# Two layers of attention over 32 images: where the turned maxima are written, when queries are scaled, and how the last image is finished

## The reference

```python
x = x + L0(_gn(x))   # _gn: group norm, 32 groups of 8 channels, no weights
x = x + L1(_gn(x))
```

```python
s = einsum('bhqe,bhke->bhqk', q, k) * scale
s = where(mask, s, finfo.min); p = softmax(s); o = einsum('bhqk,bhke->bhqe', p, v)
out = einsum('bnd,od->bno', o, Wo)
```

## Time and profile before

| what | value |
|---|---|
| time, median of 3 runs | 1193.71 us (1193.16 to 1195.25) |
| time of the profiled execution | 1191.12 us |
| its span, first to last instruction | 1189.3 us |
| TensorE busy in the span | 1118.1 us (94%) |
| VectorE busy | 929.3 us (78%) |
| ScalarE busy | 642.9 us (54%) |
| GpSimd busy | 199.4 us (17%) |
| mean granted TensorE clock | 0.981 |

### The profile page before, as it was taken

One profiled execution on the slowest core, in us unless ns is written; L12 is line 12 of the kernel. 1 busy time (PEld: TensorE's weight loads), 2 busy tenths in 40 slices (PEclk: granted clock), 3 DMA queues, 4 the chain that ended last, 5 costly groups with the idle time before them and its releaser, 6 DMA issues. The chain is left out here.

```text
span 1189.3 us, 50917 instructions
## 1 busy us (share of the span) xinstructions
PE 1118.1 (94%) x21342; PEld 826.0 (69%) x21342; DVE 929.3 (78%) x1669; ACT 642.9 (54%) x1051; POOL 199.4 (17%) x271
## 2 busy tenths in 40 slices
PE   6899999999999999988999999999999999999993
PEld 3677777777777777776667777777777777777762
DVE  5478888888888888856687887878787878787863
ACT  4456666666666666543555555555555555555550
POOL 1001111111111111111222212122221212222220
PEclk9799999999999999999999999999999999999996
DMA  2111111111111110000122222231322222222233
GB/s 87 50 33 44 41 37 37 37 37 37 37 37 37 37 38 24 24 23 10 29 49 62 54 54 58 49 70 40 69 41 66 43 64 45 63 45 62 45 70 75
DMA packets 189150, 55.49 MB, mean 47 GB/s; under 512 B 151172, under 2 KB 184214, under 8 KB 189078
## 3 DMA queue, kind: packets, MB, share of 16 engines
q1 hardware_dynamic: 182584, 52.92, 18.5%
q10 hardware_dynamic: 6496, 1.53, 0.6%
HBM read 35.95 MB, written 18.35 MB: 46 GB/s over the span
## 5 line engine op out<-in xcount | busy, mean ns | idle before, releaser
L1385 DVE TENSOR_REDUCE cm<-psG 128x4 f32<-128x1024 f32 (+1 forms) x192 | 234.9, 1224 | 115.0 <-PE psG L1109 114.9
L1255 ACT ACTIVATE probs<-psG 128x1024 f32<-128x1024 f32 x192 | 196.2, 1023 | 134.5 <-PE psG L1087 134.1
L1087 PE MATMUL psG<-stack 32*128 32x256 f32 (+1 forms) x2048 | 218.4, 342 | 8.7 <-DVE cm L1385 8.0
L1463 POOL TENSOR_SCALAR_AFFINE_SELECT probs<-probs 128x1024 f32<-128x1024 f32 x128 | 139.2, 1099 | 478.2 <-ACT probs L1255 478.1
L1096 PE MATMUL psG<-stack 32*128 32x256 f32 (+1 forms) x2048 | 219.3, 342 | 0.0
L1087 PEld LDWEIGHTS psG<-stack 32*128 32x128 f32 x2048 | 150.2, 185 | 65.7 <-DVE cm L1385 27.5
L1096 PEld LDWEIGHTS psG<-stack 32*128 32x128 f32 x2048 | 149.6, 185 | 1.3 <-issue 0.9
L885 POOL TENSOR_TENSOR X<-X,probs 128x96 f32 (+5 forms) x128 | 54.9, 459 | 482.4 <-ACT probs L625 482.4
L500 PE MATMUL psA<-probs,xh 128*128 128x512 f32 x256 | 126.8, 619 | 2.8 <-ACT xh L658 1.6
L1148 PE MATMUL psA<-xh,wqk 128*128 128x256 f32 x512 | 121.9, 382 | 0.0
L1411 DVE RECIPROCAL stack<-stack 128x128 f32<-128x128 f32 x128 | 115.7, 929 | 4.6 <-DMA stack<-totals 4.6
(11 more groups left out here) (139 smaller groups left out, 1813.1 us busy)
## 6 DMA issues: line engine op xcount, KB each, us to landing
X<-in_xr SPq DMA_DIRECT2D x32, 256.0 KB, 3.8
probs<-inverses SPq DMA_DIRECT2D x32, 256.0 KB
stack<-scratch_heads SPq DMA_DIRECT2D x32, 256.0 KB
stack<-totals SPq DMA_DIRECT2D x64, 128.0 KB
out<-X SPq DMA_DIRECT2D x32, 256.0 KB, 3.0
scratch_heads<-stack SPq DMA_DIRECT2D x124, 64.0 KB
totals<-stack SPq DMA_DIRECT2D x124, 4.0 KB
inverses<-rd SPq DMA_DIRECT2D x32, 32.0 KB, 1.5
```

The source lines that it names most:

```text
L1087: last = nc.tensor.matmul(G[:, to:to + b.size], km[i.k][own_rows(r), o, e, b.keys_of(o) * P:(b.keys_of(o) + 1) * P], qm[i.k][own_rows(r), ...
L1255: nc.scalar.activation(weights[i.k][:, b.weights_at:b.weights_at + 1024], G[:, base:base + 1024], ACT.Exp).then_inc(exp_done, 1)
L1385: nc.vector.reduce_max(slots, scores, AX_X).then_inc(max_done, 1)
L1463: nc.gpsimd.affine_select(out=diagonal, in_=diagonal, compare_op=ALU.is_ge, fill=0.0, base=0, pattern=[[0, QUADS], [0, 2], [sign, P]], cha ...
```

## The change

On TensorE `turn_c` goes behind `project` half 1 and writes the bank E; it waits for the reciprocal of the sums. The wait of `scores` for `ct` goes between its two groups of products. On ScalarE `copy_c` reads E and goes behind the second square. On VectorE `unit_qk` goes ahead of the first half of the bias. The last `output` of layer zero goes behind the last bursts. The last image's statistics go from the end of layer zero to the end of step 0 of layer one. The last image's outputs get a buffer of their own, their copies no longer wait for the stores before, and their eight stores are issued half by ScalarE and half by SyncE.

```diff
@@ def scores(i):
-                wait(pe, c_out, i.count(1))
                 wait(pe, exp_done, i.plus(-1).count(2))
...
                                                  qt[i.k][own_rows(r), o, win(w)], start=(o == 0 and w == 0), stop=False,
                                                  tile_position=(r * COL, e * WTOK), skip_group_check=True)
+                wait(pe, c_out, i.count(1))
@@ def turn_c(i):
                 wait(pe, max_done, i.count(2))
+                wait(pe, r_done, i.plus(-1).count(1))
+                if first(i):
+                    pe.wait_ge(a_tab, 1)
                 for t in range(TT):
-                    last = nc.tensor.transpose(G[:, t * P:(t + 1) * P], cm[:, t, :], ident[:, :])
+                    last = nc.tensor.transpose(E[:, t * P:(t + 1) * P], cm[:, t, :], ident[:, :])
@@ pipeline(pe, ...)
-            [... (only(LAST, bounds_begin), -1), (output, -1), (only(LAST, bounds_end), -1), (turn, 2), ...
-             (lambda i: project(i, 0), 3), (groups, 4, 1), (turn_c, 1), (lambda i: project(i, 1), 3)]
+            [... (only(LAST, bounds_begin), -1), (only(LAST, bounds_end), -1), (output, -1), (turn, 2), ...
+             (lambda i: project(i, 0), 3), (groups, 4, 1), (lambda i: project(i, 1), 3), (turn_c, 1)]
@@ def copy_c(i):
-                nc.scalar.activation(ct[:, :], G[:, 0:TOKENS], ACT.Copy, scale=-1.0).then_inc(c_out, 1)
+                nc.scalar.activation(ct[:, :], E[:, 0:TOKENS], ACT.Copy, scale=-1.0).then_inc(c_out, 1)
@@ pipeline(act, ...)
-             (lambda i: square(i, 0), 3), (bias_within, 1), (copy_c, 1), (lambda i: square(i, 1), 3)]
+             (lambda i: square(i, 0), 3), (bias_within, 1), (lambda i: square(i, 1), 3), (copy_c, 1)]
@@ def later_bounds():
                 later.take_max(WHOLE_1B)
-                stats_next(Image(0, LAST))
-                later.halves(1)
@@ pipeline(dve, ...)
-             (outputs, -1), (lambda i: add_bias(i, 0), 0), (unit_qk, 2), (prepare_bounds, 2), ...
+             (outputs, -1), (unit_qk, 2), (lambda i: add_bias(i, 0), 0), (prepare_bounds, 2), ...
@@ layer one
+    ots_last = flat[0][:, QUADS * TOKENS:2 * QUADS * TOKENS].rearrange("p (g t) -> p g t", g=QUADS)
+    def regroup_half(queue, n):
+        i = Image(0, images - 1)
+        queue.wait_ge(loaded[i.k], i.plus(-2).dmas(LOADS))
+        queue.wait_ge(ot_out[0], images)
+        queue.wait_ge(ot_out[1], images)
+        for c in (2 * n, 2 * n + 1):
+            queue.dma_start(scratch[i.k]...[:, c], ots_last[COL * c:COL * c + DIM, :, :]...).then_inc(stored[i.k], 16)
+        for g in (2 * n, 2 * n + 1):
+            queue.dma_start(totals[i.k]...[g], ots_last[DIM:P:COL, g, :]...).then_inc(stored[i.k], 16)
@@ def regroup(i):   # SyncE
             if here(i, images - 1):
+                regroup_half(sp, 1)
                 return
@@ def copy_outputs(i, o):
-            wait(act, stored[1 - i.k], i.plus(-1).dmas(STORES))
+            if not here(i, images - 1):
+                wait(act, stored[1 - i.k], i.plus(-1).dmas(STORES))
+            to = ots_last if here(i, images - 1) else ots
@@ ScalarE, in the place of regroup_last
+            regroup_half(act, 0)
@@ def last_statistics():   # VectorE, only(0, ...) at the end of the list of layer one
+            dve.wait_ge(l0.x1_done, 4 * images)
+            for c in range(CT):
+                nc.vector.bn_stats(stats2[:, images - 1, c, :], X[:, images - 1, c, :]).then_inc(l0.stats_done, 1)
+            halves(1)
```

More of the change, by code:

```diff
@@ L532, in bounds_end @@
                 later.burst(WHOLE_1B)
-            pipeline(pe, images, [(scores, 0), (project_v, 1), (bounds, 1), (only(LAST, bounds_begin), -1), (output, -1), (only(LAST, bounds_end), -1), (turn, 2), (only(LAST - 1, later.project_first), 0),
+            pipeline(pe, images, [(scores, 0), (project_v, 1), (bounds, 1), (only(LAST, bounds_begin), -1), (only(LAST, bounds_end), -1), (output, -1), (turn, 2), (only(LAST - 1, later.project_first), 0),
                                   (only(LAST, later.project_second), 0), (weigh, 0), (table_read, 0), (sums, 0), (only(LAST, lambda: later.burst(WHOLE_0)), 0),
-                                  (lambda i: project(i, 0), 3), (groups, 4, 1), (turn_c, 1), (lambda i: project(i, 1), 3)], LAGS, once={-3: hide_early, -2: hide_late, -1: tabulate})
+                                  (lambda i: project(i, 0), 3), (groups, 4, 1), (lambda i: project(i, 1), 3), (turn_c, 1)], LAGS, once={-3: hide_early, -2: hide_late, -1: tabulate})
             later.rest()
@@ L663, in _ @@
                                    (only(LAST - 1, later.queries_keys), 0),
-                                   (only(LAST, later.second_queries_keys), 0), (copy_o, 0), (lambda i: square(i, 0), 3), (bias_within, 1), (copy_c, 1), (lambda i: square(i, 1), 3)], LAGS, once={-3: rectify_early, -2: rectify_late, -1: open_table})
+                                   (only(LAST, later.second_queries_keys), 0), (copy_o, 0), (lambda i: square(i, 0), 3), (bias_within, 1), (lambda i: square(i, 1), 3), (copy_c, 1)], LAGS, once={-3: rectify_early, -2: rectify_late, -1: open_table})
             later.rest()
@@ L1232, in scalar, with regroup_first_half @@
     def scalar(act, l0):
[L1233 to L1244, removed]
+        def regroup_first_half():
+            regroup_half(act, 0)
         def exponent(i, b):
@@ L1299, in rest @@
                                    X_(HALVES), (lambda i: copy_outputs(i, 1), -1),
[L1300 removed]
+                                       (only(images - 1, regroup_first_half), -1), (copy_v, 1), X_(HALVES_B), (copy_q, 2),
                                    X_(WHOLE_1), (lambda i: copy_k(i, 0), 2), X_(WHOLE_1B)], LAGS, start=0)
@@ L1439, in rest @@
                                    R(HALVES), I_(1), I_(2), R(HALVES_B), I_(3), (divide, -2), R(WHOLE_1),
-                                   (lambda i: fold_bound(i, 0), 1), (residual, -2), R(WHOLE_1B), (only(2, lambda: roots(1)), 0)], LAGS, start=0)
+                                   (lambda i: fold_bound(i, 0), 1), (residual, -2), R(WHOLE_1B), (only(0, last_statistics), 0),
+                                       (only(2, lambda: roots(1)), 0)], LAGS, start=0)
         return VectorOpening(halves, group_sums, roots, factors, lambda: normalize(first), lambda: normalize(second),
```

11 lines of the change are left out of this document (8 added, 3 removed).

## The result

The changed kernel takes 1213.85 us, median of 4 runs (1213.46 to 1214.44), beside 1194.01 us (1193.16 to 1195.25, 4 runs) for the kernel before: ratio 1.0166, 95% interval 1.0148 to 1.0183. It is 1.7% slower, where 1185.9 us and 0.7% faster was forecast. The span of the profiled execution grew from 1189.3 to 1212.7 us, 23.4 us.

What follows compares the result with a forecast made beforehand. TensorE was taken as nearly full in layer zero's loop, its small waits winnable. Terms -5.5 - 0.2 (written-out steps) - 0.5 + 0.2 - 0.4 - 1.4 = -7.8 us put the median at 1185.9 us, range 1181 to 1191.

Steps and rivals of the forecast that it cites:

- The loop term: Layer zero's 22 loop steps: moving `turn_c` behind `project` 1 saves 0.25 us a step, -5.5 us (0 to -9.9).
- Rivals 1 to 3: Loop: ring not shortened, 1191.4 us (chance 0.14); wait inside `scores` bites, 1203.7 (0.08); more than one wait goes, 1176.0 (0.08).
- the ring: Layer zero's step as a dependency chain over TensorE, ScalarE and VectorE; `turn_c` holds it up 0.25 us a step.
- Both edits are needed together: Loop: moving `turn_c` and putting unit queries ahead of the first bias give 0.25 us a step only together.
- The wait in the middle of `scores`: Loop: `ct` awaited between the two product groups of `scores` arrives with 0.5 us to spare, cost 0.
- Rival 2: Loop: the wait inside `scores` bites, losing 1.07 us there, +10 us in all, 1203.7 us; chance 0.08.
- First image: First image of layer zero: first half of `scores` runs in its wait for `ct`, -0.5 us (0 to -1.9).
- Last two images: Layer zero, no projection to hide behind: `turn_c` waits for the reciprocal, +0.2 us (-0.5 to +0.8).
- The seam: Between layers: last bursts move up 0.85 us, output fills the wait before the full burst, -0.4 us (0 to -1.6).
- The tail: End of kernel: own buffer and split store issue let the last reciprocals start earlier, -1.4 us (-0.5 to -1.7).

Runs made afterwards that it cites:

- after_shift251: The changed kernel with 502 more waits (251 instructions) at the head of TensorE's program; 1235.56 us, ratio 1.0338.
- after_lean: The changed kernel without three TensorE waits that other waits ahead of them already cover; 1193.28 us, ratio 0.9960.
- before_shift5: The kernel before with ten more waits (five instructions) at the head of TensorE's program; 1195.23 us, ratio 1.0004.
- before_unit: The kernel before with only VectorE's order changed, unit queries and keys ahead of the first half of the bias; 1223.29 us, ratio 1.0237.
- before_lean: The kernel before without two covered TensorE waits, in `scores` and `bounds`; 1221.12 us, ratio 1.0188.
- lean_shift8: after_lean with eight extra instructions (16 waits) far ahead of the image loop; 1213.03 us, ratio 1.0150.
- lean_seam_back: after_lean with the last image's output again ahead of the second part of its bounds; 1187.48 us, ratio 0.9931.
- best: lean_seam_back with the last two images' turned maxima in the first bank again and `ct` awaited ahead of `scores`; 1185.82 us, ratio 0.9915.

## Why the prediction was wrong

**The loop term (-5.5 us; measured +17.3).** This step failed, and in two ways. The larger is not in it at all: TensorE loads nine blocks of its own code again in three turns, 20.4 us over quiet steps (with the loop's end short of the edge: 20.3 less). The prediction said of the loop that TensorE "is nearly full, but its small waits are what a reordering can win"; that the loop's 1707 instructions only just stay loaded wasn't seen, and no rival held it. Rivals 1 to 3 are all about waits between engines. What could have been seen blind: 56 packets of 16.4 KB for a program that contains a loop of seven blocks, none loaded twice, and hence something to lose.

The smaller: `turn_c` is worth 0.33 us a pair, not 0.50. From `weigh` to where `project` 1 ends takes 5.69 us instead of 5.95, as counted. But from there to the next `weigh` takes 8.76 and 9.31 instead of 8.67 and 9.21 us, since the square now starts 0.20 us behind the start of what follows `project` 1, not 0.10; the ring gives back 0.09 us a step. Over 22 steps -3.6 rather than -5.5; the six loops without slow groups and with the changed order came to -2.6 to -3.1, as their first pair was longer.

**"Both edits are needed together" was wrong.** The pairs are 29.44 and 29.45 us with either order on VectorE. In the kernel before the unit order alone gives no shorter pair; it sets off the loading.

**The wait in the middle of `scores`, cost 0:** right. No idle before L404 in the loop, and no sign of the few tenths of a us that the prediction held possible there, without a working: 126 products take 1.56 us in after, 124 took 1.53 before. Rival 2 forecast a slower kernel (1203.7 us) by a mechanism that didn't happen.

**First image (-0.5; measured -1.3):** right in sign, too small, within its range. The table's cut hides it, since `scores` now starts ahead of its wait. From the start of `project` half 0 to the bound's products (L404) it is 8.9 to 9.0 us in the five traces with the old order, 7.7 in the nine with the new. TensorE's instructions, before, then after:

```profile
51.32 1.96 PE L500 MATMUL psA<-probs,xh 128*128 128x512 f32 x4 [1.25 <-ACT stack L632]
...
60.35 0.42 PE L404 MATMUL psG<-ct,pick 32*64 32x256 bf16 x1
```
```profile
54.57 1.96 PE L500 MATMUL psA<-probs,xh 128*128 128x512 f32 x4 [0.72 <-ACT stack L635]
...
62.24 0.42 PE L404 MATMUL psG<-ct,pick 32*64 32x256 bf16 x16 [2.03 <-ACT ct L651]
```

The first products run in the wait, which leaves 2.03 us of the 3.09. That `project` itself starts 3.25 us later in after is no part of the change: it starts at 51.0 to 54.8 us with either order (after_shift251, with its longer head, aside).

**Last two images (+0.2):** the mechanism came, its price is open. `turn_c` waits 0.85 us for the reciprocal, twice. The five steps behind the loop take 70.3 to 75.5 us in the seven traces with that wait (mean 72.9), 70.4 to 71.9 in the seven without (mean 71.2), so the change may cost more than was forecast. But in the last of these steps the bound's products come 3.9 us behind the start of `sums` with the wait and 4.0 without, and "issue" of up to 2.15 us inside `scores` moves about from trace to trace; no run separates the two. The 1.92 us of "issue" ahead of L404 in one of the written-out steps of after is such a one (none to 2.00 us elsewhere, 1.23 in before).

**The seam (-0.4; measured +4.0).** The order of events came as forecast, its clock did not. In after_lean the moved bursts start at 539.34; with the lengths of the earlier trace rows at full clock the full burst would follow at 539.34 + (547.02 - 1.57 - 540.60) + 2.05 = 546.24, and it came at 551.24. The step that failed is the silence on the gap: where the output stood ahead of the bursts it filled TensorE's wait for the maximum, and I took only that the bursts "can move up by 0.85". With the output behind, TensorE idles there (1.67 us in after, 1.82 in after_lean), the granted clock falls, and bursts and output run at half speed. Over all traces that is 3.2 us. In after itself 2.2 of the +4.0 lie behind the first burst; the other 1.8 lie ahead of it, at the output that waits 4.34 us and in the projection behind it, and also vary among traces with the same order.

**The tail (-1.4; measured -1.1):** right, by its own mechanism: reciprocals right behind the residual. One term was too small: 0.2 us was taken off because the earlier stores share the DMA engines with image 30's fetch. Image 30's reciprocals start 6.5 to 6.9 us behind the last products at L1129 in the four traces with the old tail, and 6.7 to 9.0 (mean 7.7) in the ten with the new stores, 1.0 us later.

Without the slow groups and with the seam and the last images undone, the kernel comes to 1185.8 us, but by other terms than the forecast's.

**What stays open.** Why timing matters across the edge: before (end 5576) and before_shift5 (5581) load nothing twice, before_unit (5576) and before_lean (5573) load nine blocks in every second turn. The edge itself is only bracketed, between 5569 and 5573. With edges every 256 instructions from there, a loop that ends short of it lies in seven blocks and one that ends behind it in eight. That the sequencer asks for the block behind the loop and so loses the loop's first one fits every run, and the times of the packets (one, less than a microsecond later the next, then seven spread over the two steps that follow), but no packet names its block. Nor is it shown how many turns load again in a run without a trace: of each kernel one run was traced, and the runs of before reach 1203.07 us where the traced one took 1191.12.

## What to carry to other kernels

Read the packets of the instruction queue before and after a change to a kernel with a large unrolled loop: packets over the program's size are code loaded again, and equal products torn apart by 2 us of "issue" are how it looks on the engine. If a loop only just stays loaded, its place matters more than what is in it, and a change on another engine can set it off; shift it by a few instructions, and keep its end clear of the edge, before you judge a reordering. And a long operation that stands in a wait is worth more than the place that it takes: behind it the wait comes back, and with it the clock.

## What the runs showed of the hardware

One reload is nine packets and costs the loop 5.3 us (before_unit: 354.25 - 327.76 = 26.5, five of them) to 7.1 us (lean_shift8: 14.1, two). TensorE's program is that of before in before_unit. The cost is in part the clock: behind the waits of 1.92 and 2.59 us in after the 32 products at L440 take 3.03 us, 1.97 in a quiet step. A folded pair of waits on a semaphore long reached cost about 21 us / 251 = 0.08 us on TensorE. Behind an idle time of 1.82 us the granted clock was 0.50 over the ten us that follow, with TensorE busy all the time (10.00 of 10.00). With 1.56 us idle at 544.70 (lean_seam_back) it stayed at 1.00, with 1.57 at 540.47 (best) it fell, for the 3.28 us shown: the length of this one wait doesn't decide it.
